# Second copies of a serial chain moved to the scalar engine, one mask stage merged, one reload of x dropped (linear-attention block with expert FFN)

## The chip, the cores and the metric

One Trainium2 chip, all 8 cores. Each core works alone on two of the 16 sequences (4096 rows of 1024), with no traffic between cores. The time is that of the slowest core in microseconds of the device. PE is the tensor engine, DVE the vector engine, ACT the scalar engine, POOL the one that issues the weight DMAs, SP the one that issues the other DMAs.

## The reference

```python
# x: (16, 2048, 1024); 16 heads of 64; chunks of 64 rows
x = x + attn(layernorm(x))
x = x + ffn(layernorm(x))

def attn(x):
    q, k, v = x @ Wq.T, x @ Wk.T, x @ Wv.T        # per head
    k = k / max(norm(k), 1e-12)
    for each chunk of 64:
        out = softmax(causal(q k^T / 8)) v + 0.1 * q M
        for each row t of the chunk:              # delta rule
            M = M - alpha (M k_t) k_t^T + beta v_t k_t^T
    return out @ Wo.T

def ffn(x):                                       # groups of 16 rows
    perm = one-hot over the 16 rows, for each of 64 (expert, slot)
    sel = perm^T x;  inter = relu(sel f1 + bias) f2;  out = perm inter
```

## The kernel before

The first phase runs over 8 bands of 512 rows (256 of each of the two sequences). A band goes through: the load of x into x_sb, layernorm, transposes, the q, k and v projections, the solve, the chunk steps, the output projection and the store of x1 to DRAM. The recurrence over the 64 rows of a chunk is turned into a triangular solve. For each band there are four systems (two chunk pairs `cp` times two sequences `b`), each of 16 heads and two chunks side by side (128 partitions x 1024 columns). L397 and L398 form A0 and its transpose B0. Then five squaring rounds (L406 and L412, 64 matmuls of 64x64, 32 in the fifth) write psB and psC; L418 copies psB to the next A and L420 copies psC to the next B (not in the fifth). Six apply steps follow: 32 matmuls (L437) and one addition on DVE (L445, L451).

The chunk steps run 64 times (8 bands x 4 chunks x 2 sequences). PE writes scores to psA and two products with the states H and M to psB and psC (L474 to L481). ACT takes the exponential (L486), DVE applies the causal mask (L489), scales psB into tmp_f (L495) and adds v (L503, RHS). PE forms the row sums and PV (L513, L516) and then the state updates (L526, L529). DVE normalises (L533 to L544) and updates H and M (L553, L557).

The output projection (L593) takes 4 batches of 16 matmuls; after each, DVE adds x (L600). For this the band's x is loaded again by L584 and L587 into `xr_sb`, which is the same memory as `x_sb`.

The second phase runs over two halves of 2048 rows. For each of 16 tiles of 128 rows it loads x1 (L660), normalises, chooses rows (L692 to L727) and gathers them by 8 matmuls into two PSUM banks in turn (L731), each copied to sel_sb (L734). Then the expert FFN runs over 64 slots (L763, L771, L775, L781), and a scatter of 16 tiles writes the result (L806, L813).

There is no scheduler. Every stage is emitted by `Em.stage`, in order, for one engine. It waits for counts of other engines' semaphores, one wait instruction per engine, in the order of the dictionary; a count that this engine has waited for before is skipped. It returns the engine's count after all functions of the stage, and `em.cnt` is what has been emitted so far. An engine runs its own stages in the order written.

Of the kernel before, what the change touches and what calls it, by code (L numbers as in the profile page):

```python
# [10 lines left out]
ALU = mybir.AluOpType  # L11
# [69 lines left out]
def build_nc(dbg_upto=None):  # L81
# [6 lines left out]
    x_h = din("x", [TC, D])  # L88
# [27 lines left out]
    with ExitStack() as ctx:  # L116
# [19 lines left out]
        E = em.stage  # L136
# [63 lines left out]
        with ExitStack() as pa:  # L200
# [48 lines left out]
            for band in range(NBAND):  # L249
# [131 lines left out]
                for cp in range(2):  # L381
                    for b in range(2):
                        gfns = []
                        for h in range(NH):
                            hb = (h % 2) * 64
                            hr = (h % 2) * 8 + h // 2
                            col = (h // 2) * 512 + b * 256
                            for ci in range(2):
                                c = 2 * cp + ci
                                ksl = k_fm[hb:hb + 64, col + c * 64:col + c * 64 + 64]  # L390
                                gfns.append(lambda t, ksl=ksl, hr=hr, h=h, ci=ci: t.matmul(
                                    psA[ci * 64:ci * 64 + 64, hr * 64:hr * 64 + 64],
                                    ksl, ksl, start=True, stop=True,
                                    tile_position=((h % 2) * 64, ci * 64)))
                        tG = E("t", gfns, waits={"v": em.cnt["v"], "s": em.cnt["s"]})
                        vM = E("v", [
                            lambda v: v.tensor_tensor(A_bufs[0][:], psA[:, 0:1024], mA0[:], ALU.mult),  # L397
                            lambda v: v.tensor_tensor(B_bufs[0][:], psA[:, 0:1024], mB0[:], ALU.mult),  # L398
                        ], waits={"t": tG, "v": init_v})
                        if dbg_upto == "gmask":  # L400
                            break
                        for k in range(5):
                            sq_fns = []
                            for h in range(NH):
                                for par in (0, 64):
                                    sq_fns.append(lambda t, k=k, h=h, par=par: t.matmul(  # L406
                                        psB[par:par + 64, h * 64:h * 64 + 64],
                                        B_bufs[k][par:par + 64, h * 64:h * 64 + 64],
                                        A_bufs[k][par:par + 64, h * 64:h * 64 + 64],
                                        start=True, stop=True, tile_position=(par, par)))  # L410
                                    if k < 4:
                                        sq_fns.append(lambda t, k=k, h=h, par=par: t.matmul(  # L412
                                            psC[par:par + 64, h * 64:h * 64 + 64],
                                            A_bufs[k][par:par + 64, h * 64:h * 64 + 64],
                                            B_bufs[k][par:par + 64, h * 64:h * 64 + 64],
                                            start=True, stop=True, tile_position=(par, par)))
                            tS = E("t", sq_fns, waits={"v": vM})
                            ev = [lambda v, k=k: v.tensor_copy(A_bufs[k + 1][:], psB[:, 0:1024])]  # L418
                            if k < 4:
                                ev.append(lambda v, k=k: v.tensor_copy(B_bufs[k + 1][:], psC[:, 0:1024]))  # L420
                            vM = E("v", ev, waits={"t": tS})
                        kb_cols = [None, None]
                        for ci in range(2):
                            c = 2 * cp + ci
                            tl = b * 2 + c // 2
                            kb_cols[ci] = tl * 1024
                        tlp = b * 2 + cp
                        kbt = kb_tm[:, tlp * 1024:(tlp + 1) * 1024]
                        Wcur = None
                        for k in range(6):  # L430
                            ap_fns = []
                            for h in range(NH):
                                hr = (h % 2) * 8 + h // 2
                                rsl = (kbt[:, h * 64:h * 64 + 64] if k == 0
                                       else Wcur[:, hr * 64:hr * 64 + 64])
                                for par in (0, 64):
                                    ap_fns.append(lambda t, k=k, hr=hr, par=par, rsl=rsl: t.matmul(  # L437
                                        psB[par:par + 64, hr * 64:hr * 64 + 64],
                                        A_bufs[k][par:par + 64, hr * 64:hr * 64 + 64],
                                        rsl[par:par + 64, :],  # L440
                                        start=True, stop=True, tile_position=(par, par)))
                            tA = E("t", ap_fns, waits={"v": vM})
                            Wnext = W_fin[b] if k == 5 else A_bufs[k]
                            if k == 0:
                                vM = E("v", [lambda v, Wnext=Wnext, kbt=kbt: v.tensor_tensor(  # L445
                                    Wnext[:, :].rearrange("p (b a c) -> p b a c", b=2, a=8),
                                    psB[:, 0:1024].rearrange("p (b a c) -> p b a c", b=2, a=8),
                                    kbt.rearrange("p (a b c) -> p b a c", a=8, b=2),
                                    ALU.add)], waits={"t": tA}, selfdep=True)
                            else:  # L450
                                vM = E("v", [lambda v, Wnext=Wnext, Wcur=Wcur: v.tensor_tensor(  # L451
                                    Wnext[:], psB[:, 0:1024], Wcur[:], ALU.add)],
                                    waits={"t": tA}, selfdep=True)
                            Wcur = Wnext
                        if dbg_upto == "solve" and cp == 0 and b == 0:
                            break
# [4 lines left out]
                    for ci in range(2):  # L461
# [3 lines left out]
                        for b in range(2):  # L465
                            tl = b * 2 + c // 2
                            fns = []
                            for h in range(NH):
# [17 lines left out]
                            sE = E("s", [lambda s, pbase=pbase: s.activation(  # L486
                                PT_sb[pbase:pbase + 64, :], psA[pbase:pbase + 64, 0:1024],
                                AF.Exp, scale=0.125)], waits={"t": tSMm})
                            vP = E("v", [lambda v, pbase=pbase: v.tensor_tensor(  # L489
                                PT_sb[pbase:pbase + 64, :].rearrange("p (a b) -> p a b", b=64),  # L490
                                PT_sb[pbase:pbase + 64, :].rearrange("p (a b) -> p a b", b=64),
                                maskj_bf[pbase:pbase + 64, :].unsqueeze(1).broadcast_to([64, 16, 64]),
                                ALU.mult)], waits={"s": sE})
                            E("v", [
                                lambda v, pbase=pbase: v.tensor_tensor(  # L495
                                    tmp_f[pbase:pbase + 64, :].rearrange("p (b a c) -> p b a c", b=2, a=8),
                                    psB[pbase:pbase + 64, 0:1024].rearrange("p (b a c) -> p b a c", b=2, a=8),
                                    abbc[pbase:pbase + 64, 16:32].rearrange("p (a b) -> p b a", a=8)
                                        .unsqueeze(3).broadcast_to([64, 2, 8, 64]),
                                    ALU.mult),  # L500
                            ], waits={"t": tSMm})
                            vR = E("v", [
                                lambda v, tl=tl, pbase=pbase: v.tensor_add(  # L503
                                    RHS_sb[pbase:pbase + 64, :].rearrange("p (b a c) -> p b a c", b=2, a=8),
# [67 lines left out]
                for oc in range(8):  # L572
# [7 lines left out]
                    E("v", [lambda v, oc=oc: v.tensor_copy(  # L580
                        o_fm[:, oc * 512:(oc + 1) * 512], psT[:, 0:512])], waits={"t": tt})
                vOf = em.cnt["v"]
                yxr = E("y", [
                    lambda y: y.dma_start(  # L584
                        out=xr_sb[:, 0:2048].rearrange("p (n m) -> p n m", n=2),
                        in_=x_h[r0:r0 + 256, :].rearrange("(n p) m -> p n m", p=128)),
                    lambda y: y.dma_start(  # L587
                        out=xr_sb[:, 2048:4096].rearrange("p (n m) -> p n m", n=2),
                        in_=x_h[r1:r1 + 256, :].rearrange("(n p) m -> p n m", p=128)),
                ], dma=True, waits={"v": em.cnt["v"], "s": em.cnt["s"]})  # L590
                for tl in range(TPB):
                    tW = E("t", [
                        (lambda t, tl=tl, oc2=oc2, half=hf: t.matmul(  # L593
# [6 lines left out]
                    E("v", [lambda v, tl=tl: v.tensor_add(  # L600
                        x1_sb[:, tl * 1024:(tl + 1) * 1024],
                        xr_sb[:, tl * 1024:(tl + 1) * 1024],
                        psA[:, 0:1024])], waits={"t": tW, "y": yxr})
                vx1 = em.cnt["v"]
                E("y", [
                    lambda y: y.dma_start(
# [21 lines left out]
        with ExitStack() as pb:  # L628
# [27 lines left out]
            for half in range(2):  # L656
                for tl in range(16):
# [71 lines left out]
                    for kc in range(8):  # L729
                        pg = pb1 if kc % 2 == 0 else pb2  # L730
                        tg = E("t", [lambda t, kc=kc, pg=pg: t.matmul(  # L731
                            pg[:, 0:512], y_sb[:, kc * 128:(kc + 1) * 128], psel_sb[:],
                            start=True, stop=True)], waits={"v": em.cnt["v"]})
                        E("v", [lambda v, kc=kc, tl=tl, pg=pg: v.tensor_copy(  # L734
                            sel_sb[:, (kc * 16 + tl) * 512:(kc * 16 + tl) * 512 + 512],
                            pg[:, 0:512])], waits={"t": tg})
                vGather = em.cnt["v"]

                def f1_load(g, j, buf):
# [162 lines left out]
```

How the kernel before makes its waits and increments, by code:

```python
        def body(e):  # L47
            if (selfdep or dma) and own > 0 and lw.get((ek, ek), 0) < own:
                e.wait_ge(sem[ek], own)
                lw[(ek, ek)] = own
            for k, v in wl:
                if lw.get((ek, k), 0) >= v:
                    continue
                e.wait_ge(sem[k], v)
                lw[(ek, k)] = v
            run = own
            for i, f in enumerate(fns):
                if serial_dma and i > 0:
                    e.wait_ge(sem[ek], run)
                    lw[(ek, ek)] = run
                ins = f(e)
                if not noinc:
                    ins.then_inc(sem[ek], 16 if dma else 1)
                run += 16 if dma else 1
```

## Time and profile before

| | us |
|---|---|
| median of 3 runs | 5934.9 (5926.77 to 5936.67) |
| the profiled execution | 5934.46 |
| its span, slowest core (core 0) | 5932.9 |
| spans of all cores | 5910.2 to 5932.9 |
| mean granted clock of PE, all cores | 0.563 to 0.566 |
| first phase, up to about | 3730 |
| busy: PE / DVE / ACT | 2068.8 / 2049.0 / 875.4 |

The page gives each engine's busy time and groups of equal instructions. The chain of waits follows the work that ended last back through time: each piece was released by the one before it, and "issue", "DVEq" and "ACTq" are short pieces of hand-over. The order of time lists instructions with their start and length. The granted clock is a share of 2.4 GHz: 0.50 is the level of 1.2 GHz, 1.00 that of 2.4 GHz.

### The profile page before, as it was taken

Reading aid. Unit: us, or ns where it says so; the run is one execution under the profiler, and the core shown is the slowest. Engines: PE = TensorE matmul, PEld = TensorE weight load, DVE = VectorE, ACT = ScalarE, POOL = GpSimd, SP = SyncE. Lnnn points to the kernel's source line nnn. Section 1 sums busy time; section 2 is a strip of 40 time slices with the busy share of each in tenths; the row PEclk is TensorE's granted clock in tenths of the full one; section 3 lists DMA queues with packets and bytes.
Section 4 is the critical chain, followed back from the end, with each engine's and each line's share of the span. In section 5 each row is a group of like instructions: output and inputs, shape, how many; then the busy total and the mean of one; then the engine's idle time right before and its main releaser. Section 6 shows DMA issues by size and latency. Waiting matters only on the chain.

```text
span 5932.9 us, 66710 instructions; the slowest of 8 cores (5910.2 to 5932.9 us)
## 1 busy us (share of the span) xinstructions
PE 2068.8 (35%) x28832; PEld 1264.6 (21%) x28902; DVE 2049.0 (35%) x2550; ACT 875.4 (15%) x931; POOL 59.7 (1%) x85
## 2 busy tenths in 40 slices
PE   2434333433433433434434433222333222224322
PEld 0232232232232232133133133111111001111100
DVE  2343343344244244254254244333322023332210
ACT  1101201201201200200200200111232001113200
POOL 0000000000000000000000000000000000000000
PEclk9556556655655655655655755555555555555555
DMA  4000001001000000000000000000254420015544
GB/s 73 1 1 36 1 1 36 1 1 36 1 1 36 0 1 37 0 1 22 14 1 15 21 1 12 18 9 9 47 107 101 112 67 7 9 18 103 96 104 112
DMA packets 96562, 189.11 MB, mean 32 GB/s; under 512 B 6080, under 2 KB 38928, under 8 KB 92176
## 3 DMA queue, kind: packets, MB, share of 16 engines
q1 hardware_dynamic: 48384, 142.62, 8.0%
q0 software_dynamic: 47888, 42.21, 5.3%
q8 instruction: 232, 3.80, 0.3%
q14 instruction: 58, 0.48, 0.0%
HBM read 168.22 MB, written 58.72 MB: 38 GB/s over the span
## 4 chain that ended last, share of the span: by engine, by line
PE 35%; DVE 28%; DMA 16%; ACT 12%; issue 8%; DVEq 1%; SPq 0%; ACTq 0%; POOLq 0%
DMA x1t_sb<-x1d 6%; DMA interd<-inter_sb 4%; PE psB L437 4%; DVE A L418 3%; DVE sel_sb L734 3%; PE psB L406 3%; PE psC L412 3%; DVE A L451 3%; DVE B L420 2%; PE psB L326 2%; PE pb L731 2%; PE psA L313 2%; PE psC L326 2%; PE pb L806 2%; DMA x_sb<-x 2%
## 5 line engine op out<-in xcount | busy, mean ns | idle before, releaser
L406 PE MATMUL psB<-A,B 64*64 64x64 bf16 x5120 | 272.9, 238 | 499.6 <-DVE B L420 395.5
L486 ACT ACT_TABLE_LOAD x64 | 82.1, 1283 | 2012.1 <-PE psC L481 2012.1
L406 PEld LDWEIGHTS psB<-A,B 64*64 64x64 bf16 x5120 | 256.0, 151 | 516.5 <-issue 516.5
L781 DVE CAST inter_sb<-pb 128x1024 bf16<-128x1024 f32 x128 | 156.7, 1224 | 516.7 <-DMA interd<-inter_sb 264.3
L418 DVE CAST A<-psB 128x1024 bf16<-128x1024 f32 x160 | 195.9, 1224 | 389.1 <-PE psC L412 339.8
L326 PE MATMUL psB<-wk_sb,xn_fm 128*128 128x512 bf16 x504 | 180.7, 444 | 255.5 <-DVE kb_tm L354 246.1
L437 PE MATMUL psB<-A 64*64 64x64 bf16 x5120 | 170.1, 238 | 272.9 <-DVE A L451 218.4
L775 PE MATMUL pb<-f,inner_sb 64*128 64x512 bf16 x256 | 129.1, 606 | 389.5 <-ACT inner_sb L771 197.3
L806 PE MATMUL pb<-f1a,pselT_sb 128*128 128x512 bf16 x250 | 111.6, 621 | 417.0 <-DMA x1t_sb<-x1d 416.1
L734 DVE CAST sel_sb<-pb 128x512 bf16<-128x512 f32 x256 | 176.9, 691 | 215.0 <-PE pb L731 201.6
L412 PE MATMUL psC<-B,A 64*64 64x64 bf16 x4096 | 240.1, 238 | 0.0
L771 ACT ACT_TABLE_LOAD x128 | 164.2, 1283 | 496.7 <-PE pb L763 496.7
L412 PEld LDWEIGHTS psC<-B,A 64*64 64x64 bf16 x4096 | 228.1, 153 | 0.0
L451 DVE TENSOR_TENSOR A<-psB,A 128x1024 bf16<-128x1024 f32 x128 | 156.7, 1224 | 197.8 <-PE psB L437 197.8
L731 PE MATMUL pb<-psel_sb,y_sb 128*128 128x512 bf16 x240 | 140.0, 583 | 243.0 <-DVE sel_sb L734 232.2
L437 PEld LDWEIGHTS psB<-A 64*64 64x64 bf16 x5120 | 153.2, 151 | 289.8 <-issue 289.8
L813 DVE TENSOR_TENSOR yfbuf<-x1t_sb,pb 128x1024 f32<-128x1024 bf16 x32 | 39.1, 1221 | 489.6 <-PE pb L806 489.6
L513 PE MATMUL psD<-onescol,PT_sb 64*64 64x1 bf16 x1024 | 113.9, 187 | 245.0 <-DVE PT_sb L489 245.0
L663 ACT ACT_TABLE_LOAD x32 | 41.1, 1283 | 1016.7 <-DMA x1t_sb<-x1d 1016.7
L326 PE MATMUL psC<-wv_sb,xn_fm 128*128 128x512 bf16 x504 | 176.1, 434 | 0.6 <-issue 0.2
L687 PE MATMUL pbT<-ident_bf,y_sb 128*128 128x128 bf16 x256 | 32.3, 306 | 408.1 <-DVE y_sb L683 408.1
L335 DVE TENSOR_REDUCE rk_sb<-sq_sb 128x16 f32<-128x1024 bf16 x32 | 39.0, 1220 | 366.8 <-ACT sq_sb L333 366.8
(159 smaller groups left out, 4314.3 us busy)
## 6 DMA issues: line engine op xcount, KB each, us to landing
x_sb<-x SPq DMA_DIRECT2D x32, 1024.0 KB, 6.9
interd<-inter_sb SPq DMA_DIRECT2D x32, 1024.0 KB, 8.7
f1a<-interd SPq DMA_DIRECT2D x32, 1024.0 KB, 7.7
x1t_sb<-x1d SPq DMA_DIRECT2D x64, 256.0 KB, 5.2
f<-f2w POOLq DMA_DIRECT2D x32, 512.0 KB, 5.5
out<-yfbuf SPq DMA_DIRECT2D x32, 512.0 KB, 2.6
x1d<-x_sb SPq DMA_DIRECT2D x16, 512.0 KB, 3.7
f1a<-f1w POOLq DMA_DIRECT2D x16, 512.0 KB, 9.7
```

The lines of the kernel that those rows point to most:

```text
L326: (lambda t, tl=tl, kc2=kc2, which=w, half=hf: t.matmul((psB if which == 0 else psC)[:, half * 512:half * 512 + 512], xn_fm[:, kc2 * 512 + ...
L406: sq_fns.append(lambda t, k=k, h=h, par=par: t.matmul(psB[par:par + 64, h * 64:h * 64 + 64], B_bufs[k][par:par + 64, h * 64:h * 64 + 64], ...
L412: sq_fns.append(lambda t, k=k, h=h, par=par: t.matmul(psC[par:par + 64, h * 64:h * 64 + 64], A_bufs[k][par:par + 64, h * 64:h * 64 + 64], ...
L418: ev = [lambda v, k=k: v.tensor_copy(A_bufs[k + 1][:], psB[:, 0:1024])]
L437: ap_fns.append(lambda t, k=k, hr=hr, par=par, rsl=rsl: t.matmul(psB[par:par + 64, hr * 64:hr * 64 + 64], A_bufs[k][par:par + 64, hr * 64: ...
L451: vM = E("v", [lambda v, Wnext=Wnext, Wcur=Wcur: v.tensor_tensor(Wnext[:], psB[:, 0:1024], Wcur[:], ALU.add)], waits={"t": tA}, selfdep=True)
L731: tg = E("t", [lambda t, kc=kc, pg=pg: t.matmul(pg[:, 0:512], y_sb[:, kc * 128:(kc + 1) * 128], psel_sb[:], start=True, stop=True)], waits ...
L734: E("v", [lambda v, kc=kc, tl=tl, pg=pg: v.tensor_copy(sel_sb[:, (kc * 16 + tl) * 512:(kc * 16 + tl) * 512 + 512], pg[:, 0:512])], waits={ ...
L771: sR = E("s", [lambda s, es=es: s.activation(inner_sb[:], pb0[0:64, 128:256], AF.Relu, bias=biasT_sb[:, es:es + 1])], waits={"t": tF1})
L775: lambda t, hf=hf, el=el, buf=buf: t.matmul(pb3[:, hf * 512:hf * 512 + 512], inner_sb[:], f2_sb[buf][:, el * 1024 + hf * 512:el * 1024 + h ...
L781: E("v", [lambda v, el=el: v.tensor_copy(inter_sb[:, el * 1024:(el + 1) * 1024], pb3[:, 0:1024])], waits={"t": tF2, "y": em.cnt["y"]})
L806: (lambda t, k=k, hf=hf, tl=tl, po=po: t.matmul(po[:, hf * 512:hf * 512 + 512], pselT_sb[:, tl * 512 + k * 128:tl * 512 + k * 128 + 128], ...
```

## The change

There are four edits. The copy of psC to the next B moves from DVE to ACT, and the matmuls of the squaring and apply steps wait for ACT's count beside DVE's. The mask and the scaling into tmp_f become one stage of two functions, so that `vP` is the count after both. The second load of x is left out. In the gather the odd ones of the eight copies go to ACT, and each gather matmul waits for ACT's count beside DVE's.

```diff
-                            tS = E("t", sq_fns, waits={"v": vM})
-                            ev = [lambda v, k=k: v.tensor_copy(A_bufs[k + 1][:], psB[:, 0:1024])]
+                            tS = E("t", sq_fns, waits={"v": vM, "s": em.cnt["s"]})
                             if k < 4:
-                                ev.append(lambda v, k=k: v.tensor_copy(B_bufs[k + 1][:], psC[:, 0:1024]))
-                            vM = E("v", ev, waits={"t": tS})
+                                E("s", [lambda s, k=k: s.copy(B_bufs[k + 1][:], psC[:, 0:1024])],
+                                  waits={"t": tS})
+                            vM = E("v", [lambda v, k=k: v.tensor_copy(A_bufs[k + 1][:], psB[:, 0:1024])],
+                                   waits={"t": tS})
...
-                            tA = E("t", ap_fns, waits={"v": vM})
+                            tA = E("t", ap_fns, waits={"v": vM, "s": em.cnt["s"]})
...
-                            vP = E("v", [lambda v, pbase=pbase: v.tensor_tensor(
-                                PT_sb[pbase:pbase + 64, :].rearrange("p (a b) -> p a b", b=64),
...
-                                ALU.mult)], waits={"s": sE})
-                            E("v", [
+                            vP = E("v", [
+                                lambda v, pbase=pbase: v.tensor_tensor(
+                                    PT_sb[pbase:pbase + 64, :].rearrange("p (a b) -> p a b", b=64),
...
                                 lambda v, pbase=pbase: v.tensor_tensor(
                                     tmp_f[pbase:pbase + 64, :].rearrange("p (b a c) -> p b a c", b=2, a=8),
...
-                            ], waits={"t": tSMm})
+                            ], waits={"s": sE, "t": tSMm})
...
-                yxr = E("y", [
-                    lambda y: y.dma_start(
...
-                ], dma=True, waits={"v": em.cnt["v"], "s": em.cnt["s"]})
+                yxr = em.cnt["y"]
...
-                        psA[:, 0:1024])], waits={"t": tW, "y": yxr})
+                        psA[:, 0:1024])], waits={"t": tW})
...
-                            start=True, stop=True)], waits={"v": em.cnt["v"]})
-                        E("v", [lambda v, kc=kc, tl=tl, pg=pg: v.tensor_copy(
-                            sel_sb[:, (kc * 16 + tl) * 512:(kc * 16 + tl) * 512 + 512],
-                            pg[:, 0:512])], waits={"t": tg})
+                            start=True, stop=True)],
+                            waits={"v": em.cnt["v"], "s": em.cnt["s"]})
...
+                        if kc % 2 == 0:
+                            E("v", [lambda v, kc=kc, tl=tl, pg=pg: v.tensor_copy(
...
+                        else:
+                            E("s", [lambda s, kc=kc, tl=tl, pg=pg: s.copy(
```

## Rows read from the trace of the kernel before

**Rows 1.** The page: busy time by engine, and the chain's shares by engine.
```profile
PE 2068.8 (35%) x28832; PEld 1264.6 (21%) x28902; DVE 2049.0 (35%) x2550; ACT 875.4 (15%) x931; POOL 59.7 (1%) x85
...
PE 35%; DVE 28%; DMA 16%; ACT 12%; issue 8%; DVEq 1%; SPq 0%; ACTq 0%; POOLq 0%
```

**Rows 2.** Chain of waits, one squaring round: start us, us, what.
```profile
227.34 0.55 PE psC L412 x2
227.98 1.23 DVE A L418
229.21 1.14 DVE B L420
230.35 0.14 issue
...
232.99 1.22 DVE A L418
```

**Rows 3.** Groups on ACT: busy us, mean ns of one, idle before.
```profile
L360 ACT ACT_TABLE_LOAD x32 | 41.1, 1283 | 0.6
...
L360 ACT ACTIVATE v_tm<-psC 128x1024 bf16<-128x1024 f32 x32 | 32.8, 1024 | 0.4
...
L343 ACT ACTIVATE rk_sb<-rk_sb 128x16 f32<-128x16 f32 x32 | 6.9, 216 | 0.4
```

**Rows 4.** Order of time, key stage: start us, us, instruction.
```profile
145.89 1.02 ACT L360 ACTIVATE v_tm<-psC 128x1024 bf16<-128x1024 f32 x1
146.10 1.21 DVE L354 TENSOR_TENSOR kb_tm<-psB,rk_sb 128x1024 bf16<-128x1024 f32 x1
```

**Rows 5.** Chain of waits, PE's start behind kb_tm (its stage waits for v and s).
```profile
165.19 1.14 DVE kb_tm L354
166.33 0.25 issue
```

**Rows 6.** One chunk step: chain of waits, then DVE in order of time.
```profile
304.58 0.45 PE psC L481 x2
305.10 1.28 ACT L486
306.39 1.03 ACT PT_sb L486
...
308.21 0.24 issue
...
308.12 1.21 DVE L495 TENSOR_TENSOR tmp_f<-psB,abbc 64x1024 bf16<-64x1024 f32 x1
309.43 0.68 DVE L503 TENSOR_TENSOR RHS_sb<-tmp_f,v_tm 64x1024 bf16<-64x1024 bf16 x1
310.44 0.25 DVE L533 RECIPROCAL re_sb<-psD 64x16 f32<-64x16 f32 x1 [0.32 <-PE psA L516]
```

**Rows 7.** Chain of waits, one turn of the gather.
```profile
3757.26 0.14 issue
3757.40 0.60 PE pb L731
...
3758.09 0.70 DVE sel_sb L734
```

**Rows 8.** Output projection: second and third batch, and PE's pauses for L600 (us, times).
```profile
502.74 5.18 PE L593 MATMUL psA<-wo_sb,xn_fm 128*128 128x512 bf16 x16 [2.67 <-DVE x_sb L600]
...
509.40 3.61 PE L593 MATMUL psA<-wo_sb,xn_fm 128*128 128x512 bf16 x16 [1.47 <-DVE x_sb L600]
...
  DVE x_sb L600: 50.7, 24
```

**Rows 9.** Stretches: us, busy PE, PEld, DVE, ACT, POOL (instructions), granted clock, DMA share, GB/s.
```profile
217.00:242.00 25.00, 8.95 (x304) 8.29 (x295) 11.88 (x11) 0.00 (x0) 0.00 (x0) 0.50 0.01 2
...
508.00:519.00 11.00, 7.17 (x31) 2.99 (x32) 3.23 (x3) 0.00 (x0) 0.00 (x0) 1.00 0.00 0
4411.00:4425.00 14.00, 7.08 (x34) 3.13 (x35) 4.48 (x4) 4.93 (x6) 1.52 (x2) 0.50 0.37 48
```

More of the change, by code:

```diff
@@ L488, in build_nc @@
                                 AF.Exp, scale=0.125)], waits={"t": tSMm})
-                            vP = E("v", [lambda v, pbase=pbase: v.tensor_tensor(
-                                PT_sb[pbase:pbase + 64, :].rearrange("p (a b) -> p a b", b=64),
-                                PT_sb[pbase:pbase + 64, :].rearrange("p (a b) -> p a b", b=64),
-                                maskj_bf[pbase:pbase + 64, :].unsqueeze(1).broadcast_to([64, 16, 64]),
-                                ALU.mult)], waits={"s": sE})
-                            E("v", [
+                            vP = E("v", [
+                                lambda v, pbase=pbase: v.tensor_tensor(
+                                    PT_sb[pbase:pbase + 64, :].rearrange("p (a b) -> p a b", b=64),
+                                    PT_sb[pbase:pbase + 64, :].rearrange("p (a b) -> p a b", b=64),
+                                    maskj_bf[pbase:pbase + 64, :].unsqueeze(1).broadcast_to([64, 16, 64]),
+                                    ALU.mult),
                                 lambda v, pbase=pbase: v.tensor_tensor(
@@ L582, in build_nc @@
                 vOf = em.cnt["v"]
-                yxr = E("y", [
-                    lambda y: y.dma_start(
[L585 to L589, printed above, removed]
-                ], dma=True, waits={"v": em.cnt["v"], "s": em.cnt["s"]})
+                yxr = em.cnt["y"]
                 for tl in range(TPB):
@@ L732, in build_nc @@
                             pg[:, 0:512], y_sb[:, kc * 128:(kc + 1) * 128], psel_sb[:],
-                            start=True, stop=True)], waits={"v": em.cnt["v"]})
-                        E("v", [lambda v, kc=kc, tl=tl, pg=pg: v.tensor_copy(
-                            sel_sb[:, (kc * 16 + tl) * 512:(kc * 16 + tl) * 512 + 512],
-                            pg[:, 0:512])], waits={"t": tg})
+                            start=True, stop=True)],
+                            waits={"v": em.cnt["v"], "s": em.cnt["s"]})
+                        ek2 = "v" if kc % 2 == 0 else "s"
+                        if kc % 2 == 0:
+                            E("v", [lambda v, kc=kc, tl=tl, pg=pg: v.tensor_copy(
+                                sel_sb[:, (kc * 16 + tl) * 512:(kc * 16 + tl) * 512 + 512],
+                                pg[:, 0:512])], waits={"t": tg})
+                        else:
+                            E("s", [lambda s, kc=kc, tl=tl, pg=pg: s.copy(
+                                sel_sb[:, (kc * 16 + tl) * 512:(kc * 16 + tl) * 512 + 512],
+                                pg[:, 0:512])], waits={"t": tg})
                 vGather = em.cnt["v"]
```

## The prediction

> **What bounds the kernel now.** I read the page first. No engine is full: PE is busy 35% of the span, DVE 35%, ACT 15%, and the chain that ended last is made of turns, PE 35%, DVE 28%, DMA 16%, ACT 12% [rows 1]. Every stage waits for the one before it, so the time of this kernel is a sum of stage lengths and hand-overs, and an edit is worth what it does to one link, times the number of links. So I went through the four places that the diff touches, in the chain of waits and in the order of time.
>
> The squaring rounds of the solve come first. A round is: both evictions on DVE one after the other (1.23 then 1.14 us on the chain), 0.14 us until PE starts, and the matmuls up to the next eviction; 5.01 us in all [rows 2]. PE waits for both copies, DVE waits for PE, and nothing else runs.
>
> **Part 1: B's eviction goes to ACT (128 times: 8 bands x 4 systems x 4 rounds).** DVE is left with A. ACT's copy of this size is not in the trace. The nearest row is the v_tm eviction, 128x1024 f32 from PSUM to bf16, at 1024 ns [rows 3], against DVE's 1.23 us [rows 2]. ACT starts 0.07 us after PE's last matmul ends (304.58 + 0.45 = 305.03, and ACT at 305.10) [rows 6], DVE 0.09 us after it (227.34 + 0.55 = 227.89, and DVE at 227.98) [rows 2]. So ACT is done 0.07 + 1.03 = 1.10 us after the matmuls, counting 1.03 us as the chain does for the exponential of the same width, and DVE 0.09 + 1.23 = 1.32 us after them: A is the later one, and the 1.14 us of B leave the chain. Do the two disturb each other in PSUM? In the key stage ACT reads psC while DVE reads psB; both keep their lengths, 1.02 and 1.21 us [rows 4].
>
> What is late next is PE's start. It waited for one semaphore, and now waits for two, v and then s. With one wait the hand-over from DVE to PE is 0.14 us [rows 2]. Where two are due, it is 0.25 us after kb_tm [rows 5] and 0.24 us ahead of the PV products [rows 6]. I take 0.11 us for the second one; without it the part gains 14 us more. A round thus saves 1.14 - 0.11 = 1.03 us: **-132 us**. The apply steps (L437) get an s wait too, but the fifth squaring has met it before them: it costs nothing.
>
> The large unknown is a table load. Every stage of ACT that calls an activation shows one of 1283 ns ahead of it, and so does the v_tm stage, whose function is Copy (32 of 32) [rows 3]. The change calls `s.copy`, not an activation with a function; no row shows that form. The ends are 0 and 1.28 us. The stage nearest in size has the load. But its call names a function of the activation tables and the new one names none, and a load in front of it would have nothing to bring. So I take 0, and the other end is a rival with a chance of its own. The Trainium skill says in "ScalarE: Activation LUTs" (section "Table sets: the hidden batching unit") that the cheap functions, copy among them, are in every set, so that no switch would be needed for one; the v_tm rows do not agree with it, since each has its load. By the rule the sum stays at the forecast below, by those rows it is the first rival's. The section "What ACT_TABLE_LOAD costs" puts a switch at about 2.66 us with its drain; here the activation follows 0.01 us after a load of 1.28 us, so this trace does not agree with that either, and with the page's figure the load rival would come out 256 x 1.38 = 353 us later still, an estimate from that page.
>
> **Part 2: the mask and tmp_f become one stage (64 times).** The order on DVE stays: the mask (L489), tmp_f (L495), RHS (L503). What moves is the count that PV's matmuls wait for: vP was the mask's, and is now tmp_f's. Before, the mask ends, PE starts PV 0.24 us later, and tmp_f (1.21 us), then RHS, run on DVE under it [rows 6]. The reciprocal starts at 310.44, just behind PV's last product, since DVE had waited for it; RHS had ended at 310.11. So PV sets when the reciprocal starts, and from there DVE works without a break to the end of the step. After the change PE can't start before tmp_f ends: 309.33 instead of the mask's end at 308.20, that is 1.13 us later, and so is the reciprocal. Nothing absorbs it: DVE has only RHS to do in that time, did it early before, and now idles behind it. The state update's products (L526, L529) move by the same amount and stay under the two long DVE operations. Cost 64 x 1.13 = **+72 us**. The mask itself now waits for s and t where it waited for s alone; t is long met. By PE's second wait that is up to 0.11 us each, 0 to +7 us; the boundary between the mask and tmp_f, where a wait stood before, was hidden (they overlap by 0.07 us), so I take +7. Together **+79 us**.
>
> **Part 3: x is not loaded again (8 bands, two DMAs of 1 MB each).** x_sb still holds the band's x, and x1's first addition no longer waits for the y queue. Behind that addition PE waits with the second batch of output products. PE's 24 pauses for L600 are 50.7 us in all, and an undisturbed pause is 1.47 us [rows 8]: 50.7 - 24 x 1.47 = 15.4 us. One matmul record in sixteen is missing in each first batch; were it the last one, PE was busy up to 0.4 us longer, 3 us in all. I take 14. Second, after the long pause the second batch takes 5.18 us where the third takes 3.61 [rows 8]. The later batches had a granted clock of 1.00, the level of 2.4 GHz [rows 9], and their pauses of 1.47 us did not lower it; at the level of 1.2 GHz sixteen products would take 7.2 us, so 5.18 us is a batch that began on the lower level. Seven of the eight bands show this. With a pause like those, 7 x 1.57 = 11 us come back; the ends are 0 and 11, and the nearest rows, the third batches, speak for 11. Together **-25 us**. SP loses two issues; the store of x1 behind them waits for v anyway.
>
> **Part 4: every second gather copy goes to ACT (128 times: 2 halves x 16 tiles x 4).** It looks like two engines in turn, but each matmul still waits for all copies emitted before it, so the turns stay one after the other. A turn is 0.14 + 0.60 + 0.09 + 0.70 = 1.53 us, and from 3757.26 to the copy's end at 3758.79 it is the same [rows 7]. On ACT: its 16-column operation takes 216 ns and its 1024-column one 1024 ns [rows 3], so 512 columns by an even slope take 216 + 496 x 0.80 = 0.61 us, an estimate. The turn is 0.14 + 0.60 + 0.07 + 0.61 = 1.42 us, 0.11 less; 128 of them give -14 us. The first matmul of each of 32 tiles now meets two new counts, v and s: +0.11 each, +4 us. If ACT hands over to PE 0.11 us more slowly than DVE, the part is worth nothing; the ends are -14 and +4. I take **-10 us**.
>
> **The sum.** -132 + 79 - 25 - 10 = -88 us. The profiled execution took 5934.5 us (span 5932.9), the median of the runs is 5934.9, so the two can be used alike: 5934.5 - 88 = 5846.5, say **5847 us**.
>
> **Rivals.**
> *A table load ahead of each `s.copy`* (the other side). In the solve ACT then ends at 0.07 + 1.28 + 1.03 = 2.38 us, plus 0.14 to PE: 2.52 against the old 0.09 + 1.23 + 1.14 + 0.14 = 2.60, so -10 us instead of -132. In the gather 128 x 1.28 = +164 us on top of -10. Sum -10 + 79 - 25 + 154 = +198: 6132 us. For it speaks the v_tm stage [rows 3]; against it, that the call differs. It decides from a load of about 0.45 us: 0.22 us of slack in the solve are free, and beyond it each 0.1 us costs 26 us. Chance 10%.
> *The two evictions don't overlap*, because PSUM gives one engine after the other its turn. Then part 1 saves nothing: -132 becomes about 0, 5979 us, slower too; it decides where A and B together last 0.7 us longer than A alone. The overlapping rows of the key stage speak against it [rows 4]. Chance 3%.
> *PV is not held back*, because something else, not seen in these rows, already keeps PV's end where it is: 5847 - 72 = 5775 us. That DVE now waits for PV with RHS done 0.33 us earlier speaks against it [rows 6]. Chance 3%.
> *The clock rises in the solve.* The rounds now go at 0.50, with PE busy 8.95 of 25.00 us [rows 9]. From PE's start, 230.35 + 0.14, to 232.90 a round has 2.41 us of matmuls [rows 2]; at the upper level half of it at most comes back, 128 x 1.2 = 154 us, 5693 us. What speaks for it is that the same matmuls come 1.03 us closer together each round. Against it: in the stretch of the expert FFN PE was busy 7.08 of 14.00 us, more than the rounds will be, and was granted 0.50 as well [rows 9]. Chance 2%.
>
> **How the numbers follow.** The forecast has 80%. Its own range: part 1 down by 14 if the second wait is free, part 2 by 7, part 3 up by 14, part 4 from -4 to +14, and some 10 us for what a new instruction form may do to start and end: 5815 to 5890. The four rivals take 18%, and 2% are for losses that happen to cancel the gain; I let the range run to 5810 and 5900, which leaves them outside. A measurement here tells 0.2%, 12 us, from no change. Faster is the forecast, PV free and the clock: 85%. Slower is the load and the serial evictions: 13%. The same: 2%.
>
> **What would show it.** Right: L420's copies on ACT near 1.02 us, starting within 0.05 us of A's; a squaring round of 3.98 us; PE's start 0.25 us after A; PV starting 0.24 us after tmp_f instead of the mask, with DVE idle about 1.4 us (0.33 + 1.13) ahead of the reciprocal; no pause for a DMA at the first x1 addition and no first pause above 1.5 us; gather turns of 1.53 and 1.42 us in alternation. Wrong: ACT_TABLE_LOAD rows at the new copies, A's copy longer than 1.3 us, or ACT's copy longer than 1.25 us, from which it is the later one.

## The result, and the profile after

The changed kernel takes 6146.07 us (median of 8 runs, 6132.73 to 6154.79) against 5931.06 us for the kernel before (8 runs, 5924.61 to 5943.99). The ratio is 1.0359, 95% interval 1.0345 to 1.0373: 3.6% slower, where I had forecast 5847 us, 1.5% faster. It is 14 us above the first rival's 6132 us.

The page of the changed kernel, the lines that answer to [rows 1], and those of its groups on ACT and DVE that the change touched (busy us, mean ns of one, idle before and its releaser):

```profile
PE 2056.9 (33%) x28902; PEld 1253.9 (20%) x28902; DVE 1815.9 (30%) x2294; ACT 1408.6 (23%) x1443; POOL 59.7 (1%) x85
...
PE 34%; DVE 23%; ACT 20%; DMA 15%; issue 8%; DVEq 1%; SPq 0%; ACTq 0%; POOLq 0%
...
L419 ACT ACT_TABLE_LOAD x128 | 164.2, 1283 | 926.0 <-PE psC L412 926.0
...
L735 ACT ACT_TABLE_LOAD x128 | 164.2, 1283 | 565.1 <-PE pb L725 565.1
...
L419 ACT CAST B<-psC 128x1024 bf16<-128x1024 f32 x128 | 129.6, 1012 | 1.4
...
L735 ACT CAST sel_sb<-pb 128x512 bf16<-128x512 f32 x128 | 75.0, 586 | 1.4
```

DVE lost 233 us of work and ACT gained 533: 205 us of copies and 328 us of table loads, 128 ahead of the copies of B and 128 ahead of those of the gather. The copies themselves are as short as reckoned (1012 and 586 ns; the prediction had 1.03 us for the large one and 0.61 us, an estimate, for the small one). ACT's share of the chain went from 12% to 20%.

The chain of waits through one squaring round of the changed kernel (start us, us, what), against [rows 2]:

```profile
224.35 0.55 PE psC L412 x2
224.97 1.28 ACT L419
226.26 1.02 ACT B L419
227.28 0.14 issue
227.42 0.26 PE psB L406 x2
...
229.90 1.28 ACT L419
```

The link is now load, copy, start of PE: a round of 4.93 us where it was 5.01. A's copy on DVE has left the chain. The second wait costs nothing here (0.14 us from ACT's end to PE's start): PE waits for v first, which is long met, and is released by s.

The chain through one chunk step, and DVE in order of time there, against [rows 6]:

```profile
309.37 0.68 DVE PT_sb L491
310.05 1.15 DVE tmp_f L496
311.19 0.25 issue
311.44 0.18 PE psD L514
```

```profile
322.43 0.68 DVE L491 TENSOR_TENSOR PT_sb<-PT_sb,maskj_bf 64x1024 bf16<-64x1024 bf16 x1 [4.58 <-ACT PT_sb L487]
323.04 1.21 DVE L496 TENSOR_TENSOR tmp_f<-psB,abbc 64x1024 bf16<-64x1024 f32 x1
324.36 0.68 DVE L504 TENSOR_TENSOR RHS_sb<-tmp_f,v_tm 64x1024 bf16<-64x1024 bf16 x1
326.50 0.25 DVE L534 RECIPROCAL re_sb<-psD 64x16 f32<-64x16 f32 x1 [1.46 <-PE psB L527]
```

tmp_f is a link of the chain now, between the mask and the row sums. DVE idles 1.46 us ahead of the reciprocal, where it was 0.32. (The row names L527 as the releaser, but the stage waits for the count of the row sums and PV, L514 and L517.)

The chain through two turns of the gather, against [rows 7]:

```profile
3800.64 0.60 PE pb L725
3801.31 1.28 ACT L735
3802.60 0.60 ACT sel_sb L735
3803.20 0.14 issue
3803.33 0.60 PE pb L725
3804.03 0.70 DVE sel_sb L731
3804.73 0.14 issue
```

A turn with ACT takes 2.69 us, one with DVE 1.53 as before. In the output projection the row for PE's pauses became

```profile
  PE psA L587: 35.4, 24
```

that is 1.475 us each, against 50.7 us in 24 pauses [rows 8].

The stages by the starts of DVE's instructions, in us, each profile's slowest core. "Solve" runs from A0 to the last addition, summed over 32 systems; "chunk steps" from the last addition of the solve to the last update of M of the four steps behind it, over 16 such groups; "output projection" from the last update of M to the last addition of x, 8 bands; "gather" from a tile's pselT to the next tile's first reduction, 30 of 32 tiles; "FFN" from the first to the last copy to inter_sb, both halves. The last three columns are experiments of the next section.

| stage | before | changed | before, ACT in one block | changed, ACT in one block | the last kernel of that set |
|---|---|---|---|---|---|
| solve | 1297.3 | 1289.1 | 1297.7 | 1169.9 | 1169.7 |
| chunk steps | 755.5 | 836.8 | 673.3 | 754.7 | 674.3 |
| output projection | 282.5 | 250.4 | 286.5 | 255.9 | 256.1 |
| routing, up to pselT | 496.3 | 496.7 | 374.9 | 375.8 | 375.8 |
| gather | 465.4 | 605.0 | 463.7 | 450.6 | 293.6 |
| FFN | 639.6 | 655.7 | 536.4 | 530.0 | 506.0 |

Before to changed: -8, +81, -32, 0, +140 (and 9 more for the last tiles of the two halves together), +16; with small differences elsewhere that makes the 210 us between the two profiles.

### The profile page after: what moved, and what is told of

Same layout as the page of the kernel before. It is cut to its first block, busy times and chain, and to the rows that moved or that the text cites. A ratio compares the mean times of both kernels' runs of the same rounds, so it can differ in the third digit from the quotient of the medians.

```text
span 6142.9 us, 67282 instructions; the slowest of 8 cores (6116.6 to 6142.9 us)
## 1 busy us (share of the span) xinstructions
PE 2056.9 (33%) x28902; PEld 1253.9 (20%) x28902; DVE 1815.9 (30%) x2294; ACT 1408.6 (23%) x1443; POOL 59.7 (1%) x85
## 4 chain that ended last, share of the span: by engine, by line
PE 34%; DVE 23%; ACT 20%; DMA 15%; issue 8%; DVEq 1%; SPq 0%; ACTq 0%; POOLq 0%
DMA x1t_sb<-x1d 5%; DMA interd<-inter_sb 5%; PE psB L438 4%; PE psB L406 3%; PE psC L412 3%; ACT L419 3%; ACT L735 3%; DVE A L452 3%; PE pb L725 2%; PE psB L326 2%; PE psA L313 2%; PE psC L326 2%; ACT B L419 2%; PE psA L587 2%; PE pb L807 2%
## 5 line engine op out<-in xcount | busy, mean ns | idle before, releaser
L421 DVE CAST A<-psB 128x1024 bf16<-128x1024 f32 x160 | 195.8, 1224 | 524.4 <-PE psC L412 441.3
L782 DVE CAST inter_sb<-pb 128x1024 bf16<-128x1024 f32 x128 | 156.7, 1224 | 537.8 <-DMA interd<-inter_sb 280.0
L514 PE MATMUL psD<-onescol,PT_sb 64*64 64x1 bf16 x1024 | 114.1, 188 | 325.9 <-DVE tmp_f L496 325.9
L452 DVE TENSOR_TENSOR A<-psB,A 128x1024 bf16<-128x1024 f32 x128 | 156.7, 1224 | 198.5 <-PE psB L438 198.5
L731 DVE CAST sel_sb<-pb 128x512 bf16<-128x512 f32 x128 | 88.5, 691 | 369.6 <-PE pb L725 369.6
```

The costliest lines, as they stand in the source:

```text
L421: vM = E("v", [lambda v, k=k: v.tensor_copy(A_bufs[k + 1][:], psB[:, 0:1024])], waits={"t": tS})
L782: E("v", [lambda v, el=el: v.tensor_copy(inter_sb[:, el * 1024:(el + 1) * 1024], pb3[:, 0:1024])], waits={"t": tF2, "y": em.cnt["y"]})
```

## The experiments

### Each part alone

Four kernels, each the kernel before with one part of the diff and nothing else, so that their diffs are pieces of the one shown above.

```diff
# part 1 alone: B's copy on ACT
-                                ev.append(lambda v, k=k: v.tensor_copy(B_bufs[k + 1][:], psC[:, 0:1024]))
+                                E("s", [lambda s, k=k: s.copy(B_bufs[k + 1][:], psC[:, 0:1024])],
...
# part 4 alone: the odd gather copies on ACT
+                        else:
+                            E("s", [lambda s, kc=kc, tl=tl, pg=pg: s.copy(
...
# part 2 alone: mask and tmp_f in one stage
-                                ALU.mult)], waits={"s": sE})
-                            E("v", [
...
# part 3 alone: no second load of x
-                yxr = E("y", [
...
+                yxr = em.cnt["y"]
```

> Only part 1: B's copy of the squaring rounds on ACT, all else as before. Load theory (each s.copy, in a stage of its own, has a table load of 1.28 us ahead of it): ACT is done 0.07 + 1.28 + 1.02 = 2.37 us after the matmuls and PE starts 0.14 us later, 2.51 against 2.60 us before, so 128 x -0.09 = -11 us, a time just below that of the kernel before. Rival 1 (my forecast: the load is there but hidden, and the loss comes from the other parts): -132 us. Rival 2 (the two engines slow each other in PSUM as well): a round longer than 5.01 us, and a time above that of before.

> Only part 4: the odd gather copies on ACT. Load theory: every odd turn takes 1.28 us more and 0.11 us less for the shorter copy, so 128 x 1.17 + 4 = +154 us. Rival (the loss of the whole change sits in the solve or the chunk steps): between -14 and +4 us.

> Only part 2: the mask and tmp_f as one stage. Theory: PV's products start 1.13 us later and the mask up to 0.11 us later in each of 64 chunk steps, +72 to +79 us. Rival (PV has room on PE, as a reader of the diff may think, since no instruction is added): 0 us.

> Only part 3: the second load of x left out. Theory: 14 us of waiting for the transfer and up to 11 us of batches at the lower clock, -14 to -25 us. Rival (the transfer is hidden under the first batch of products): 0 us.

| part alone | us | before, same chip | ratio (95%) |
|---|---|---|---|
| 1 | 5931.0 | 5933.0 | 0.9998 (0.9985 to 1.0010) |
| 4 | 6087.3 | 5933.0 | 1.0274 (1.0248 to 1.0301) |
| 2 | 6033.8 | 5933.0 | 1.0172 (1.0132 to 1.0213) |
| 3 | 5944.4 | 5933.0 | 1.0016 (1.0004 to 1.0028) |

Part 1 changes nothing that the times can tell: 2 us less, where the load theory had 11 less, just outside the interval (9 less to 6 more). Its round is the 4.93 us of the changed kernel, load ahead of the copy, and its solve takes 1290.9 us, 6 less. Its forecast without a load, -132 us, is out. Part 4 costs 154 us, the load theory's figure; that it agrees to the microsecond is luck, since the interval is 147 to 179 us. Part 3 loses 11 us (2 to 17) where I had 14 to 25 of gain. Part 2 costs 101 us in the median, but its four runs lie apart: 6009.9, 6012.7, 6054.9 and 6072.2 us. The first two cost 77 and 80 us, as forecast, and the interval, 78 to 126 us, holds the 79 too. In the traces both parts do in their own stage what was forecast: the chunk steps grew from 755.5 to 837.4 us with part 2, the output projection shrank from 282.5 to 256.4 with part 3. What differs beyond that lies in a stage that neither touches. These are the copies to inter_sb, first of before, then with part 2, then with part 3 (each in the profile of its slowest core):

```profile
L781 DVE CAST inter_sb<-pb 128x1024 bf16<-128x1024 f32 x128 | 156.7, 1224 | 516.7 <-DMA interd<-inter_sb 264.3 <-PE pb L775 249.2 <-PE pb L763 3.1
```

```profile
L781 DVE CAST inter_sb<-pb 128x1024 bf16<-128x1024 f32 x128 | 156.7, 1224 | 550.4 <-DMA interd<-inter_sb 297.9 <-PE pb L775 249.3 <-PE pb L763 3.1
```

```profile
L774 DVE CAST inter_sb<-pb 128x1024 bf16<-128x1024 f32 x128 | 156.7, 1224 | 527.8 <-DMA interd<-inter_sb 275.2 <-PE pb L768 249.5 <-PE pb L756 3.1
```

DVE waited 34 and 11 us longer for the store of the block just written. It is not so on every core: the profiled execution of part 2 is one of its two long ones (6054.9 us), and in it cores 0, 1, 4 and 5 waited 258 to 261 us (before: 254 to 273 on the eight cores), and cores 2, 3, 6 and 7, the four with the longest spans, 275 to 298. That of part 3 is the shortest of its eleven (5932.4 us). The next five runs ask whether this wait is the difference.

### The first phase alone

The second phase (routing, gather, FFN, scatter) is left out in all three, and x1 is copied to the output instead; the kernels differ in the part named.

```diff
-        with ExitStack() as pb:
...
+        E("g", [lambda g: g.dma_start(out=out_h, in_=x1_d)], dma=True, waits=em.snap())
```

> The first phase of the kernel before alone; the second phase (routing, gather, expert FFN, scatter) is left out and x1 is copied to the output. A reference for the two runs below: about 3730 us plus one copy of 16 MB.

> The first phase alone with part 2 (mask and tmp_f merged). The part measured +102 us in the whole kernel, against 82 us in the rows of the chunk steps. Theory (the rest is the expert FFN, which takes longer on the slowest core when the cores meet there in another order): +76 to +84 us over the first phase of before. Rival (the merged stage costs more in the chunk steps than the rows say): +100 us.

> The first phase alone with part 3 (no second load of x). The part measured +9 us in the whole kernel. Theory (it gains what was forecast in the output projection, and the expert FFN of the slowest core takes it back): -14 to -25 us under the first phase of before. Rival (the gain is lost in the first phase itself, at the next band's load of x): 0 us or more.

The +102 and +9 us in two of these texts are the parts' costs as they stood then, 101 and 11 in the table above.

Measured: 3816.0 us for before (3811.3 to 3819.1), 3900.9 with part 2 (3898.7 to 3904.1), 3802.2 with part 3 (3799.2 to 3807.0). Part 2 costs 85 us, a little above the 76 to 84 of its theory, and part 3 gains 14, the low end of its own. Neither rival holds (+100; 0 or more). For part 3 the remainder of 25 us therefore arises in the second phase. For part 2 a remainder of 16 us is not clear of the spread of its four runs. With the sizes of the first phase the four parts make -2 + 154 + 85 - 14 = +223 us, with the medians in the whole kernel -2 + 154 + 101 + 11 = +264; the change measured +215.

The traces also show why part 3 gains 14 us and not 25. On the mean of the eight cores the output projection is 27 us shorter (258.1 against 284.7), but the seven stretches from a band's last x1 addition to the next band's A0 are 13 us longer together (1117.8 against 1104.3). In such a stretch the q projection runs 8 batches of 8 matmuls. A batch takes 3.6 us at a granted clock of 0.50 and 1.9 us at 1.00. Without part 3, 7.5 of the 56 batches of a core are of the long kind, with it 12.0, and their lengths sum to 7.5 us more. The whole kernel shows the same, 8.1 batches without and 13.0 with part 3, and so do the two kernels with two buffers of the next runs, 9.0 and 12.4. Where the other parts change too it need not: the changed kernel has 10.3, the two one-block kernels 10.8 (before) and 7.4 (changed). Here is the second batch of one band on core 0, first before (granted clock 1.00), then with part 3 in the whole kernel (0.50):

```profile
1947.37 1.89 PE L313 MATMUL psA<-xn_fm,wq_sb 128*128 128x512 bf16 x8 [0.94 <-DVE q_fm L320]
```

```profile
1929.50 3.57 PE L313 MATMUL psA<-xn_fm,wq_sb 128*128 128x512 bf16 x8 [0.94 <-DVE q_fm L320]
```

Why the clock rises later with part 3 is not shown.

### Two buffers for inter_sb

DVE writes one buffer while the other is stored, so that its wait for the store is hidden.

```diff
-            inter_sb = pb.enter_context(nc.sbuf_tensor("inter_sb", [128, 4096], BF16))
+            inter_b = [pb.enter_context(nc.sbuf_tensor(f"inter_sb{i}", [128, 4096], BF16)) for i in range(2)]
...
+                    inter_sb = inter_b[j % 2]
...
-                          waits={"t": tF2, "y": em.cnt["y"]})
+                          waits={"t": tF2, "y": ys[j]})      # the store of block j - 2
```

> The kernel before with two buffers for inter_sb in the expert FFN, so that DVE no longer waits for the store of the block just written (32 stores, 264 us of DVE's waiting in the profile of before). A reference for the next run. A block of four slots then lasts four turns of 4.0 us or the two weight loads of 16 us, instead of 19.8 us: -80 to -120 us.

> The same with part 3 (no second load of x). Theory (what part 3 gains in the first phase, 14 us when that phase runs alone, is lost in the whole kernel to longer landings of the inter stores, on which DVE waits): with that wait hidden the gain shows, 10 to 25 us under the run before this one. Rival (the loss comes from elsewhere in the second phase, the weight loads or the scatter): no gain, or up to 10 us above it.

Measured: 5832.4 us without part 3 (5830.5 to 5835.6) and 5817.6 us with it (5811.5 to 5820.1): 15 us less, the 14 us of the first phase. The first of the two, a kernel with two buffers and no other edit, is 101 us (1.7%) faster than before (ratio 0.9829, 0.9815 to 0.9842), where 80 to 120 us were expected. Its row shows the wait gone:

```profile
L783 DVE CAST inter_sb<-pb 128x1024 bf16<-128x1024 f32 x128 | 156.7, 1225 | 404.2 <-PE pb L777 392.5 <-DMA interd<-inter_sb 8.5 <-PE pb L765 3.2
```

With the wait hidden, part 3's gain in the first phase reaches the whole kernel: so the exposed store took it back. For part 2 no run with two buffers was made; that its long runs come from the same wait is argued from its rows, not shown. Why the transfers land later there (9.6 us median with part 2, 9.2 with part 3, 8.7 before, each on the slowest core) is not shown. That the eight cores then store at other times relative to each other would fit, and wasn't tried.

### ACT's stages in one block of code

Does a table load belong to the operation or to the place where it stands? `Em.stage` opens a new block of code for each stage. Here ACT's stages are collected and written into one block per phase. Operations, waits and order are the same on every engine.

```diff
-        getattr(self.block, self.ENG[ek])(body)
+        if ek == "s":
+            self.pend.append(body)
+        else:
+            getattr(self.block, self.ENG[ek])(body)
...
+    def flush(self):                       # at the end of each phase
+        pend, self.pend = self.pend, []
+        self.block.scalar(lambda e: [f(e) for f in pend] and None)
```

> The kernel before, with all of ACT's stages of a phase written into one block of code instead of one block each; same operations, waits and order on every engine. Load theory, first half (the table load belongs to the block in which an ACT operation stands, not to the operation): most of the 465 loads are gone and the time falls by the loads on the chain, at least the exponential's and half of the expert FFN's, (64 + 64) x 1.28 = 164 us, at most 465 x 1.28 = 595 us. Rival (each ACT operation brings its load wherever it stands): no change.

> The changed kernel with all of ACT's stages of a phase in one block of code. Load theory, second half: the loads ahead of the 256 moved copies are gone, and against the kernel before in the same form the four parts give what I forecast without a load, -132 + 81 - 25 - 14 = -90 us, so this run is 60 to 120 us below the run of that one. Rival (the moved copies cost for another reason, as PSUM or hand-overs): this run stays 150 to 215 us above it.

The kernel before in this form takes 5450.4 us (5437.2 to 5475.9), ratio 0.9183 (0.9148 to 0.9219): 482 us less. In the kernel before, a function that only repeats itself has a load each time: in the chunk steps ACT runs nothing but Exp, and in the FFN nothing but Relu.

```profile
L486 ACT ACT_TABLE_LOAD x64 | 82.1, 1283 | 2012.1 <-PE psC L481 2012.1
L771 ACT ACT_TABLE_LOAD x128 | 164.2, 1283 | 496.7 <-PE pb L763 496.7
```

In the one-block form these are all the table loads that the trace has left (idle before, and its releaser, at the end):

```profile
L175 ACT ACT_TABLE_LOAD x1 | 1.3, 1283 | 34.3 <-DMA gmask_sb<-gmask 34.3
L292 ACT ACT_TABLE_LOAD x1 | 1.3, 1283 | 2.3 <-DVE st_sb L291 2.3
L672 ACT ACT_TABLE_LOAD x1 | 1.3, 1283 | 51.6 <-DMA x1t_sb<-x1d 51.6
```

Three instead of 465, for Sigmoid, Square, Ln, Exp, Relu and the Copy of v_tm together: one at the start of each of the two blocks (L175, the Sigmoid, and L672) and one at the first Ln (L292). The load belongs to the block, and within a block only to a change of function. Another cost of opening a block, gone together with the load, is a rival, and the chunk steps, with one load on the chain of each step, leave little for it: they fell from 755.5 to 673.3 us, which is 1.28 us for each of 64, the length of the load.

The changed kernel in this form takes 5343.1 us (5323.4 to 5391.3), ratio to before 0.9010 (0.8958 to 0.9062): 107 us below the kernel before in the same form, inside the 60 to 120 expected. The rival (150 to 215 us above) is out. Its chain through two squaring rounds:

```profile
240.91 1.23 DVE A L429
242.15 0.24 issue
242.39 0.26 PE psB L414 x2
244.25 0.55 PE psC L420 x2
244.90 1.23 DVE A L429
246.13 0.25 issue
```

and ACT in order of time beside it:

```profile
240.90 1.01 ACT L427 CAST B<-psC 128x1024 bf16<-128x1024 f32 x1 [26.61 <-PE psC L420]
244.88 1.01 ACT L427 CAST B<-psC 128x1024 bf16<-128x1024 f32 x1 [2.98 <-PE psC L420]
```

This is the round that the prediction drew: both copies at once and neither longer for it (DVE 1.22 us, ACT 1.01), A the later, PE's start 0.24 us behind A because it waits for two engines, 3.99 us in all (forecast 3.98). The gather's turns are 1.53 and 1.41 us, and the chunk steps cost 81 us as they do with the loads: 754.7 against 673.3.

### The loads gone, the merge undone, the gather's banks used

```diff
-                            waits={"v": em.cnt["v"], "s": em.cnt["s"]})
+                            waits=gw8)          # the copy that last read this bank; for kc == 0 both counts
...
+                        last[kc % 2] = {ek2: em.cnt[ek2]}
```

Beside this edit the mask and tmp_f are separate stages, as before.

> ACT in one block; parts 1 and 3 of the change; the mask and tmp_f separate as before; and each gather matmul waits only for the copy that last used its own PSUM bank. Theory: against the changed kernel in one block PV starts 1.13 us earlier in 64 steps and the mask 0.07 us, -77 us; and a pair of gather turns falls from 1.53 + 1.42 us to about 1.55 us, set by one bank's turn, 128 x -1.4 = -180 us; together -257 us. Rival for the gather (the two engines' copies can't overlap): -77 us only.

Measured: 5089.4 us (5073.6 to 5127.8), ratio to before 0.8582 (0.8531 to 0.8633), and 254 us below the run before it, where 257 was expected. The chunk steps gave 80 us (77 expected) and the gather 157 in 30 tiles and 9 in the other two (180 expected). The FFN, which this edit doesn't touch, is 24 us shorter in its profile, so the close sum is in part luck. The two copies of the gather overlap now:

```profile
3496.77 0.69 DVE L742 CAST sel_sb<-pb 128x512 bf16<-128x512 f32 x1 [0.84 <-PE pb L736]
3497.18 0.59 ACT L746 CAST sel_sb<-pb 128x512 bf16<-128x512 f32 x1 [0.94 <-PE pb L736]
...
3498.30 0.69 DVE L742 CAST sel_sb<-pb 128x512 bf16<-128x512 f32 x1 [0.83 <-PE pb L736]
```

A pair of copies takes 1.53 us where a pair took 2.94. This kernel beats both, by 14% and 17%.

## Why the prediction was wrong

**The step that failed** is the value taken for the large unknown of part 1: "I take 0" for the table load ahead of `s.copy`. It measured 1.28 us, 256 times out of 256. The argument was that a call which names no function brings no load. The trace of the kernel before had said it otherwise: 465 loads for 466 activations, with 8 Exps in a row in each band and 64 Relus in a row in each half, are no sign of functions that change. They are one load for each stage of ACT, whatever it does; the one pair of activations that shares a load is the one pair that shares a stage (L167 and L168). The prediction saw the load ahead of every stage and still tied it to the function that is called. The nearest row, v_tm's, was the better witness, and the prediction put it aside for a reason from the code. The load turned the -10 us of the gather into +154 and the -132 us of the solve into -8, and these two shifts, 288 us, are nearly all of the 299 us between the forecast and the result. A chance of 10% for it was low for what the nearest row showed.

The Trainium skill says in "ScalarE: Activation LUTs" (section "Table sets: the hidden batching unit") that tables are loaded as sets, with the cheap functions in every set. The kernels with ACT in one block agree: Relu and Copy have no load of their own there. Its section "What ACT_TABLE_LOAD costs" adds a drain of about 1.38 us to the load. No row here shows it: a load taken off the chunk steps gave 1.28 us, and the 462 loads taken off in all gave 482 us, 1.04 us each.

**The first rival's sum** was right in its large terms. It had -10 for the solve (the trace: -8), +154 for the gather (+154 alone), +79 for the chunk steps (+81 in the trace, +85 in the first phase alone). Its -25 for the reload was not: -14 in the first phase, +11 in the whole kernel. That its 6132 us come within 14 us of the result is in part luck.

**Part 1, apart from the load**: right. 1.14 us of B's copy leave the chain, 0.11 us of a second wait come on, the engines don't disturb each other. Its -132 us are -128 in the trace of the one-block kernels.

**Part 2**: right. The moved count costs 1.13 us a step and the mask's second wait 0.07 us: before, ACT's end to the mask was 0.09 us, in the changed kernel it is 0.16 (309.21 to 309.37). Alone in the whole kernel its four runs cost 77 to 139 us; what they have above 85 is not settled.

**Part 3**: right in its own place, where the stage lost 26 to 32 us against the 25 forecast, and too large as a term of the sum: the first phase gains 14 us, and the whole kernel loses 11. The prediction ended its account at the last x1 addition. It had nothing for the next band, whose projections start with more batches at the lower clock, nor for the FFN's exposed store, which takes the rest of the gain.

**Part 4**: the turns are right (1.53 and 1.41 us without the load, and 13 us less in 30 tiles of the one-block kernels), and the copies stay serial, because every matmul waits for all copies emitted so far.

**The other rivals**: evictions that don't overlap, PV not held back, and a risen clock are all out. In the one-block form of the changed kernel, where the rounds are 1 us shorter, the solve stays on the level of 1.2 GHz: the granted clock from 238 to 250 us is 0.50, and the matmuls of a round keep their length (242.39 to 244.80, 2.41 us).

## What to carry to other kernels

Count an overhead row by the place where it stands as well as by what follows it. A load in front of every stage of an engine, needed or not, will stand in front of the next stage that is added there too, and it can be had back by writing the engine's stages into one block. A count returned after two functions delays everyone who needed only the first: merging stages without adding an instruction made the chunk steps 81 us longer here. And an exposed transfer, such as the store of inter_sb, makes the gain of an edit elsewhere hard to read; hide it first, or time the phase alone. A stage's gain is not the kernel's until the stage behind it has been looked at too.

## What was not expected of the hardware

ACT's plain copy from PSUM (1012 ns for 128x1024, f32 to bf16) runs beside DVE's (1224 ns) from another PSUM tensor with neither longer for it. A wait of PE on a second engine that stands behind the one that releases it costs 0.11 us even when it is long met (0.25 against 0.14 us), and one of DVE 0.07 us; where the last wait is the one that releases PE, the hand-over is 0.14 us. A 1 MB store landed 8.7, 9.2 or 9.6 us after its issue (medians of 32, slowest cores) in kernels that differ only in an earlier phase. Of a core's 56 batches of the q projection, 7.5, 8.1 and 9.0 took 3.6 us at a granted clock of 0.50 in three kernels with the second load of x, and 12.0, 13.0 and 12.4 in the same kernels without it; the others took 1.9 us at 1.00.
